# Two row tiles of 64 rows in place of one 128-row product, with a four-part sum, in a LoRA and FFN kernel on one core

## The reference

```python
w = weight[adapter_ids]                      # 8 of 16 weights, 1024 x 1024
y = jnp.einsum('bsi,boi->bso', x, w)         # the first product
t = y.reshape(b * l, Dm)[:, perm].reshape(b * l, h, d)
t = jnp.einsum('bhd,hdm->bhm', t, up)        # 16 heads, 64 -> 256
t = jax.nn.gelu(t, approximate=False)
t = jnp.einsum('bhm,hmd->bhd', t, down)      # 256 -> 64
return x + t.reshape(b * l, h * d)[:, unperm].reshape(b, l, Dm)
```

## Time and profile before

| what | value |
|---|---|
| median of 3 runs | 297.78 us (297.61 to 297.8) |
| span of the profiled execution | 296.1 us |
| PE busy | 290.6 us, 98% |
| VectorE busy | 179.2 us, 61% |
| ScalarE busy | 159.9 us, 54% |
| GpSimd busy | 98.8 us, 33% |
| TensorE clock granted | full in all slices |

### The profile page before, as it was taken

One profiled execution on the slowest core, in us unless ns is written; L12 is line 12 of the kernel. 1 busy time (PEld: TensorE's weight loads), 2 busy tenths in 40 slices (PEclk: granted clock), 3 DMA queues, 4 the chain that ended last, 5 costly groups with the idle time before them and its releaser, 6 DMA issues.

```text
span 296.1 us, 4358 instructions
## 1 busy us (share of the span) xinstructions
PE 290.6 (98%) x1694; PEld 215.0 (73%) x1694; DVE 179.2 (61%) x211; ACT 159.9 (54%) x179; POOL 98.8 (33%) x92
## 2 busy tenths in 40 slices
PE   8999999999999999999999999999999999999994
PEld 7788888888888838886488855888468885444441
DVE  3599679589778455973658726685446523343333
ACT  5655453466764368344584265822853207777750
POOL 4000000068552007860527007702473405222234
PEclk9999999999999999999999999999999999999999
DMA  7999999999988947799576973876752864421335
GB/s 206 363 402 421 395 421 422 366 320 375 394 328 277 378 153 197 281 360 406 212 249 196 345 311 114 312 237 199 244 191 83 286 185 122 128 71 71 144 142 212
DMA packets 23699, 77.87 MB, mean 263 GB/s; under 512 B 2688, under 2 KB 11264, under 8 KB 18816
## 3 DMA queue, kind: packets, MB, share of 16 engines
q1 hardware_dynamic: 7056, 43.39, 39.3%
q0 software_dynamic: 7488, 25.18, 24.7%
q10 hardware_dynamic: 9136, 9.05, 8.8%
HBM read 60.82 MB, written 16.78 MB: 262 GB/s over the span
## 4 chain that ended last, share of the span: by engine, by line
PE 95%; DMA 2%; SPq 1%; POOL 1%; issue 0%; DVE 0%; ACT 0%; POOLq 0%; DVEq 0%
PE ps L641 38%; PE ps L645 19%; PE ps L698 19%; PE ps L674 6%; PE ps L677 5%; PE ps L680 5%; PE ps L606 2%; DMA w_raw<-w 2%; PE ps L611 1%; POOL out_late L319 1%; SPq L223 1%; SPq L251 0%; DVE w_raw L528 0%; ACT w_hi L429 0%; POOLq L361 0%
## 5 line engine op out<-in xcount | busy, mean ns | idle before, releaser
L641 PE MATMUL ps<-x_pair,w_hi 128*128 128x512 f32 x480 | 131.5, 395 | 0.0
L381 ACT ACTIVATE w_hi<-w_raw 128x1024 fp32r<-128x1024 f32 x58 | 58.3, 1056 | 62.8 <-PE ps L645 51.6
L415 ACT ACTIVATE hidden<-ps 128x1024 f32<-128x1024 f32 x64 | 61.6, 1028 | 55.1 <-PE ps L680 47.1
L641 PEld LDWEIGHTS ps<-x_pair,w_hi 128*128 128x128 f32 x480 | 82.0, 189 | 12.8 <-issue 1.8
L645 PEld LDWEIGHTS ps<-x_pair,w_lo 128*128 128x128 f32 x480 | 73.6, 189 | 10.2
L490 DVE TENSOR_TENSOR w_lo<-w_raw,w_hi 128x1024 fp32r<-128x1024 f32 x60 | 71.0, 1222 | 11.8 <-ACT w_hi L381 10.7
L645 PE MATMUL ps<-x_pair,w_lo 128*128 128x256 f32 x480 | 76.3, 281 | 0.0
L292 POOL DMA_INDIRECT t_raw<-y_rows,idx x32 | 34.9, 1090 | 115.1 <-DMA y_rows<-y_out 82.4
L518 DVE TENSOR_REDUCE y_out<-ps 128x256 f32<-128x512 f32 x64 | 42.8, 685 | 24.5 <-PE ps L645 23.0
L698 PE MATMUL ps<-hidden,down_sb 128*64 128x512 f32 (+1 forms) x264 | 57.4, 583 | 0.0
L510 DVE TENSOR_TENSOR t_lo<-t_raw,t_hi 128x512 fp32r<-128x512 f32 x32 | 21.7, 694 | 47.9 <-ACT t_hi L405 42.5
(11 more groups left out here) (29 smaller groups left out, 119.4 us busy)
## 6 DMA issues: line engine op xcount, KB each, us to landing
w_raw<-w SPq DMA_DIRECT2D x29, 1024.0 KB
y_rows<-y_out ACTq DMA_DIRECT2D x32, 256.0 KB
x_raw<-x_cols SPq DMA_DIRECT2D x7, 1024.0 KB
w_raw<-w SPq DMA_DIRECT2D x4, 256.0 KB, 5.0
w_raw<-w SPq DMA_DIRECT2D x2, 512.0 KB, 7.7
hidden<-up SPq DMA_DIRECT2D x1, 1024.0 KB, 12.3
down_sb<-down SPq DMA_DIRECT2D x1, 1024.0 KB, 12.3
w_raw<-w SPq DMA_DIRECT2D x2, 384.0 KB, 6.9
```

The costliest lines, as they stand in the source:

```text
L381: nc.scalar.activation(w_hi[:, g % WS, k, :], w_raw[:, g % WRAW, k, :], ACT.Copy).then_inc(w_hi_done, 1)
L415: nc.scalar.activation(hidden[:, f % HS, m, :, :], up_banks(f, m)[:, :, :], ACT.Gelu).then_inc(gelu_done, 1)
L641: nc.tensor.matmul(acc, w_hi[:, ws, k, col], x_pair[:, xs, k, :, :], start=(k == 0), stop=False)
```

## The change

From unit 2 on, each product of the first product is made in two row tiles of 64 rows: rows 0 to 63 and rows 64 to 127 of the same w and x slices, each with its own matmul and its own bank (y_tiles(g, o) is a whole tensor of two banks). So a unit holds four banks, two units have banks at a time, and the sum over the rows that the array made itself is now left to the reduction: y_sum adds four parts (1024 values in, 256 out) for units 2 to 31. Units 0 and 1 stay as they are, in other banks (first_bank). The waits for free banks are now one for each o, and up_unit waits for the two units that last used its banks for each m.

```diff
+        def y_set(g):
             q = g // QUAD
+            return (max(q, LEAD) + g + (q <= LEAD)) % 2
+        def first_bank(g, o):
+            return ps[2 * y_set(g) + 1][:, o, :].rearrange("p (c s) -> p c s", c=2)
+        def y_tiles(g, o):
+            return ps[2 * y_set(g) + o].rearrange("p r (c s) -> p r c s", c=2)
...
+                    else:
+                        nc.vector.tensor_reduce(y_out[:, g % YS, o, :], y_tiles(g, o).rearrange("p r c s -> p s r c"),
+                                                mybir.AxisListType.XY, ALU.add).then_inc(y_summed, 1)
...
-                if q > LEAD:
-                    f = PAIR * 2 * (q - LEAD - 1) + g % QUAD // 2
-                    pe.wait_ge(gelu_done, MT * f + g % 2 + 1)
-                elif q == LEAD:
-                    pe.wait_ge(y_summed, OT * (g - QUAD + 1))
-                elif q > 0:
-                    pe.wait_ge(y_summed, OT * (g - 1 if g % QUAD < 2 else g - 5))
                 for o in range(OT):
                     col = slice(o * P, (o + 1) * P)
-                    acc = y_bank(g, o)
+                    acc = y_tiles(g, o)
+
+                    if g < QUAD:
+                        if o == 1:
+                            pe.wait_ge(y_summed, OT * (g - PAIR + 1))
+                    elif q > LEAD and g % QUAD < PAIR:
+                        pe.wait_ge(gelu_done, MT * (PAIR * 2 * (q - LEAD - 1) + g % QUAD) + o + 1)
+                    else:
+                        pe.wait_ge(y_summed, OT * (g - PAIR) + o + 1)
...
                         for k in ks:
-                            nc.tensor.matmul(acc, w_hi[:, ws, k, col], x_pair[:, xs, k, :, :], start=(k == 0), stop=False)
+                            for r in range(2):
+                                own = slice(r * ROWS, (r + 1) * ROWS)
+                                nc.tensor.matmul(acc[:, r, :, :], w_hi[own, ws, k, col], x_pair[own, xs, k, :, :],
+                                                 start=(k == 0), stop=False)
...
                         for k in ks:
-                            last = nc.tensor.matmul(acc[:, 0, :], w_lo[:, ws, k, col], x_hi[:, xs, k, :], start=False, stop=(k == KT - 1))
+                            for r in range(2):
+                                own = slice(r * ROWS, (r + 1) * ROWS)
+                                last = nc.tensor.matmul(acc[:, r, 0, :], w_lo[own, ws, k, col], x_hi[own, xs, k, :],
+                                                        start=False, stop=(k == KT - 1))
...
-                if behind_quad:
-
-                    pe.wait_ge(y_summed, OT * (QUAD * q + 2 * (f % 2 + 1)))
-                elif f % 2 == 1:
+                if not behind_quad and f % 2 == 1:
...
+                    if behind_quad:
+
+                        pe.wait_ge(y_summed, OT * (QUAD * q + PAIR + f % 2) + m + 1)
```

More of the change, by code:

```diff
@@ L28 @@
 HALF = KT // 2
+ROWS = P // 2
 NL = B * LPB
@@ L200, in down_bank @@
             return ps[2 * ((p + 1 - TURNS + BLOCKS) % 2)][:, f % 2, :]
-        def y_bank(g, o):
+        def y_set(g):
             q = g // QUAD
-            return ps[2 * ((q + g % QUAD // 2 + (q == LEAD)) % 2) + g % 2][:, o, :].rearrange("p (c s) -> p c s", c=2)
+            return (max(q, LEAD) + g + (q <= LEAD)) % 2
[3 more added lines that the diff above has]
+            return ps[2 * y_set(g) + o].rearrange("p r (c s) -> p r c s", c=2)
         def token_parts(f):
@@ L517, in y_sum @@
                     dve.wait_ge(lora_done, OT * g + o + 1)
-                    nc.vector.tensor_reduce(y_out[:, g % YS, o, :], y_bank(g, o).rearrange("p c s -> p s c"),
-                                            mybir.AxisListType.X, ALU.add).then_inc(y_summed, 1)
+                    if g < PAIR:
+                        nc.vector.tensor_reduce(y_out[:, g % YS, o, :], first_bank(g, o).rearrange("p c s -> p s c"),
+                                                mybir.AxisListType.X, ALU.add).then_inc(y_summed, 1)
+                    else:
+                        nc.vector.tensor_reduce(y_out[:, g % YS, o, :], y_tiles(g, o).rearrange("p r c s -> p s r c"),
+                                                mybir.AxisListType.XY, ALU.add).then_inc(y_summed, 1)
             def add_x(f):
@@ L605, in first_lora_piece @@
                     for k in ks:
-                        nc.tensor.matmul(y_bank(g, o), w_hi[:, g, k, col], x_pair[:, 0, k, :, :], start=(k == 0), stop=False)
+                        nc.tensor.matmul(first_bank(g, o), w_hi[:, g, k, col], x_pair[:, 0, k, :, :], start=(k == 0), stop=False)
                 pe.wait_ge(first_w_lo[g], n + 1)
@@ L610, in first_lora_piece @@
                     for k in ks:
-                        last = nc.tensor.matmul(y_bank(g, o)[:, 0, :], w_lo[:, g, k, col], x_hi[:, 0, k, :], start=False, stop=(k == KT - 1))
+                        last = nc.tensor.matmul(first_bank(g, o)[:, 0, :], w_lo[:, g, k, col], x_hi[:, 0, k, :], start=False, stop=(k == KT - 1))
                     if n == PIECES - 1:
```

## The result

The changed kernel takes 301.19 us (300.75 to 301.64, four runs) where the one before takes 297.69 (297.53 to 297.8): 1.0115 times as long, 95% interval 1.0101 to 1.013. The profiled execution has a span of 299.6 us (before 296.1). Slower was forecast, and 301.19 us lies inside the range given (296.5 to 302.5); but the change is +3.5 us where +1.2 was worked out, so two thirds of it were not foreseen.

A forecast was written before the change was run, and what follows sets the result against it. PE, 95% of the chain, was taken as the bound. 296.1 us +2.9 (before quad 3) +0.57 (quad 3) -1.6 (switches) -0.7 (pairs) gave 297.3, and 1.7 for the runs' median made 299.0 us; range 296.5 to 302.5.

The forecast's parts named there:

- VectorE's chain: VectorE's queue from unit 2: each four-part sum takes 1.22 us, 0.535 more, delaying later jobs until TensorE waits.
- Unit 2 to quad 3: First two up units wait for t_low(0) and y_sum(11), so quad 3 starts at 80.8 instead of 77.89: +2.9 us.
- quad 3: Late ACT and VectorE work in quad 3 delays gelu(2) and so down_unit(0): +0.57 us, switch included.
- The 0.1 us for loading weights into an empty array: Before up_unit(1), after its wait for y_sum(11): 0.1 us assumed for loading weights before the matmuls go on.
- the switches: Passages between 128-row matmuls and up_unit lose 0.20 us each, which goes: 2.0 us at most, 1.6 in quads 4 to 7.
- rival 4: The switch does not go, because the gap belongs to up_unit's start: +1.6 us, 300.6 us; chance 0.1.
- slack in the chain through ACT: Sign of a wrong forecast: ACT's chain of y_park, w_high and x_high has slack that was not seen; no size given.
- the pace of a pair: 64-row pairs in units 2 to 31: 512 columns save 0.003 us each, 0.7 us in quads 4 to 7; 256 columns unchanged.
- rival 3: TensorE cannot be fed: at 57 ns an instruction a 256-column pair takes 0.229 us, +54 us, some 350 us; chance 0.07.
- gelu is ready 0.1 to 0.2 us ahead of down_unit: Passage from up_unit to down_unit in quads 4 to 7: gelu is in time, so no wait, though little is left.
- nothing for the last part: Behind quad 7, to the last down_unit: the sum of the forecast has no term for this stretch.
- Rival 1: VectorE keeps up because the four-part sum costs only some 0.15 us more: no wait, 292.7, measured 294.4 us; chance 0.16.

The follow-up runs named there:

- half_sum: Changed kernel, but from unit 2 on the reduction adds only the first row tile's two parts (output not the full product): 295.86 us, ratio 0.9937.
- park_behind: Changed kernel with ScalarE's y_park of each quad's last unit, from quad 3 on, moved behind the first up unit's gelu: 299.35 us, ratio 1.0049.
- reordered_3: Third run of park_behind with x_low(3) and w_low(12) put behind y_sum(11) on VectorE: 302.64 us; the two earlier runs 305.34 and 302.7 us.
- half_sum_early: Changed kernel, but in units 2 to 11 only the sum leaves out the second row tile's parts (not the full product): 302.96, 302.18 and 298.35 us.
- late_tiles: Changed kernel with units 2 to 11 left as whole products with two-part sums, row tiles only in units 12 to 31: 298.41 us, ratio 1.0022.

## Why the prediction was off

**Right: VectorE's chain.** The chain held step by step. The sum takes 1.215 us (1.22 forecast), two of them 2.35. x_low(3), y_sum(10), t_low(0) and y_sum(11) start 0.4 to 0.5 us after the forecast's times, 0.36 of which is the later start of unit 2. Unit 2 to quad 3 costs +2.91 us, 2.9 forecast, and quad 3 +0.49, 0.57 forecast. The 0.1 us for loading weights into an empty array had no row behind it; from the end of the job that TensorE waits for to the matmul, weights included, the three waits here show 0.06 to 0.15 us.

**Right: the switches.** half_sum shows -0.39 us a round, 0.40 forecast, so rival 4 is out. The Trainium skill (TensorEngine Tiling (Array Packing), Key Properties) says that a change of tiling mode drains TensorE. The trace agrees as far as it goes: the 0.20 us at each passage went with the change of mode.

The forecast names three things that would make it wrong: a reduction not near 1.2 us, slack in the chain through ACT, a 256-column pair not at 0.117 us. None of them came. It failed at three other steps, each worth 0.6 to 0.7 us of the 2.3 us missed.

**Wrong: the pace of a pair (-0.7 us, measured 0).** The forecast took 0.229 from up_unit against 0.2325 from the whole matmuls. Eight matmuls in four pairs take 0.93 us in the changed kernel (118.47 to 119.40) and four pairs of 256 columns 0.47 (118.00 to 118.47), as the whole ones did. The 0.003 us belongs to up_unit and not to tiles: its pairs step by 0.23 us on average before and after, the first product's tile pairs by 0.2335. For 256 columns the forecast's 0.117 held (0.1187 on average, 0.1185 before), and rival 3 did not come. The Trainium skill (TensorE: Matmul & The Clock Gate, Part 1) has 62 ns per matmul without hardware decode, an estimate of 0.124 us for a pair. The trace has 0.1187, so nothing of it is seen here; whether decoding was in hardware no run shows.

**Wrong: "gelu is ready 0.1 to 0.2 us ahead of down_unit" in quads 4 to 7.** The four rounds gave -0.85 us and not -2.3. Of the 1.45 missing, 0.7 is the pace above. The rest is the passage up to down, 0.48 us for 0.32 at each round: a wait that the forecast put at nothing. A margin of 0.1 to 0.2 at the end of a count of a dozen steps is no margin; it should have been an even chance of a wait. park_behind shows that the y_park in front of gelu was its cause.

**Wrong: nothing for the last part (measured +0.62).** The forecast's sum stopped at quad 7, without a reason. The last four-part sum still stands ahead of four steps there, and its delay comes out at up_unit(21). park_behind takes this away too.

**Chance: +0.36** from a later start of unit 2 in the profiled execution, which this forecast could not hold. That the time fell into the range, with an estimate 2.2 us too low, is owed to a range 6 us wide.

Together: 1.2 forecast, +0.7 pace, +0.7 waits before down_unit, +0.6 last part, +0.4 start, -0.1 quad 3, which gives 3.5. Rival 1 (VectorE keeps up) decided at 0.83 us a sum, and the sum was 1.215; half_sum, at 0.685, is what it would have looked like: 295.9 us, where the rival had 294.4, because the pace's gain was counted in it as well.

## What to carry to other kernels

Row tiles do not make matmuls faster when the same columns are streamed; they save the switch where the neighbours are tiled as well, 0.2 us each here, and hand the sum over the rows to another engine. Count what that engine's longer job does to everything queued behind it on every engine, to the end of the program, and treat a margin under a few tenths of a microsecond as a likely wait. Before moving a job to a later place, ask what it frees, not only who reads its result.

## What the runs showed of the hardware that was not expected

**TensorE's clock fell behind some standstills, and not behind others.** reordered_3, windows of 2 us (busy time of PE, PEld, DVE, ACT, POOL; granted clock; DMA share; GB/s), around the wait above:

```profile
94.00:96.00 2.00, 0.97 (x8) 0.45 (x6) 2.00 (x3) 0.65 (x1) 0.00 (x0) 0.98 0.40 155
96.00:98.00 2.00, 1.96 (x14) 1.77 (x16) 2.00 (x2) 1.36 (x2) 0.00 (x0) 0.50 0.29 99
98.00:100.00 2.00, 2.00 (x20) 1.73 (x18) 2.00 (x3) 0.00 (x0) 0.00 (x0) 0.67 0.76 221
100.00:102.00 2.00, 2.00 (x26) 1.74 (x24) 2.00 (x3) 0.00 (x0) 0.00 (x0) 1.00 0.96 390
```

After two gaps of 2.6 and 1.5 us in the steps of the matmuls the granted clock is 0.50 for 96 to 98 us and 0.67 on average for the next two, the lower of the two levels (1.2 GHz), while TensorE is busy again. In half_sum_early the same follows the gap before 79.23 us, and its quad 3 takes 24.07 us instead of 22.43: 1.6 us on top of the wait. In its repeat a gap of the same length (2.0 us between two matmuls' starts) left the clock at full. The changed kernel's waits of 0.95 and 1.26 us did not lower it; in the second run of the reordered kernel two gaps of 1.36 and 1.63 us did. What decides it is not shown.

**The landing of one transfer can come some 4 us late.** The first gather waits for y_rows of units 0 to 7. From the issue of unit 7's to the gather 5.3 to 8.9 us pass in all other traces and 13.2 us in late_tiles, whose y_rows had gone out at its usual time (52.74 us). What held it up is not shown.

**Still open.** half_sum_early took 303.0, 302.2 and 298.35 us on three chips, and the changed kernel 301.19 on one and 303.28 on another, in the long ones with signals of finished matmuls seen late (by 2.3 us at gelu(0) above) or standstills of up to 1.1 us between two matmuls in which TensorE waited for no semaphore that the profile shows. The median of the kernel before did not differ between those chips (297.6 to 297.8), though single executions of it on the first two took up to 305.65 us. Row tiles make TensorE's instructions many more, 2654 matmuls for 1694, and the fetches of instructions, 21 packets of some 16 KB for 13; that they make the kernel sensitive to how fast instructions arrive would fit, and is argued, not shown.
